# Two convolution taps placed later, a copy placed before an update, and two PSUM homes exchanged in the KDA stage

## What is computed

```
q = l2norm(silu(conv4(x @ Wq)));  k = l2norm(silu(conv4(x @ Wk)));  v = silu(conv4(x @ Wv))
g = -exp(A_log) * log1p(exp(clip(x @ Wfa @ Wfb + dt_bias, -20, 20)));  beta = sigmoid(x @ Wb)
for each token i and head:                      # 16 heads of 128
    state = state * exp(g_i)
    state = state + (beta_i * k_i) (v_i - k_i . state)
    o_i   = q_i . state
out = rmsnorm(o) * norm_w * sigmoid(x @ Wga @ Wgb) @ Wo
```

## Time and profile before

| | us |
|---|---|
| median of 3 runs | 7070.68 (7065.52 to 7080.7) |
| the profiled execution | 7072.26 |
| its span | 7070.4 |
| loop over 32 KDA blocks, 2534 to 5158 us in the span | 2624 |
| PE busy in the span | 5833.4 (83%) |
| DVE, ACT, POOL busy | 3136.2, 2846.3, 2260.3 |
| granted clock of PE, mean of the span; of the loop | 0.885; 0.92 |

### The profile page before, as it was taken

How to read it: one execution, slowest core, us unless ns; L and a number is a source line. 1 busy time by engine, 2 the same in 40 slices (tenths; PEclk the granted TensorE clock), 3 DMA queues, 4 the chain that set the end, 5 groups by cost and what they waited for, 6 DMA issues and landing times. The chain is left out here.

```text
span 7070.4 us, 126135 instructions
## 1 busy us (share of the span) xinstructions
PE 5833.4 (83%) x52984; PEld 3848.7 (54%) x52984; DVE 3136.2 (44%) x4540; ACT 2846.3 (40%) x5154; POOL 2260.3 (32%) x1583
## 2 busy tenths in 40 slices
PE   6877789754899678888888888888889997888999
PEld 5666566543566345555555555555544445665444
DVE  5545333323332255555555555655532115664211
ACT  2322334333343354554454455454531115664111
POOL 4444000001000046555566655656522220001222
PEclk8988788877778789999999999999989998889999
DMA  0000000000000000000000000000021110002111
GB/s 26 3 3 31 0 0 0 14 0 29 0 0 0 9 20 15 15 15 22 15 15 15 15 15 15 22 15 15 15 82 42 42 40 1 0 0 78 42 41 46
DMA packets 60570, 136.55 MB, mean 19 GB/s; under 512 B 11638, under 2 KB 24054, under 8 KB 58842
## 3 DMA queue, kind: packets, MB, share of 16 engines
q1 hardware_dynamic: 60122, 129.79, 5.5%
HBM read 127.26 MB, written 2.50 MB: 18 GB/s over the span
## 5 line engine op out<-in xcount | busy, mean ns | idle before, releaser
L569 PE MATMUL ps<-moe_xn_all,moe_w 128*128 128x512 f32 x1792 | 810.3, 595 | 0.0
L1688 POOL TENSOR_TENSOR kda_g<-kda_g,kda_f 128x512 f32<-128x512 f32 x225 | 422.7, 1879 | 500.6 <-DVE kda_rows L1680 493.9
L569 PEld LDWEIGHTS ps<-moe_xn_all,moe_w 128*128 128x128 f32 x1792 | 341.2, 191 | 423.9 <-issue 423.3
L682 DVE TENSOR_TENSOR moe_h<-moe_silu,ps 128x512 f32<-128x512 f32 x224 | 154.1, 688 | 935.8 <-ACT moe_silu L624 928.8
L1511 DVE SCALAR_TENSOR_TENSOR kda_cv<-kda_pre,kda_w_front,kda_cv 128x1024 f32<-128x1024 f32 x297 | 545.2, 1836 | 3.6
L1399 PE MATMUL ps<-kda_xn_all,kda_w_front 128*128 128x512 f32 x808 | 428.1, 679 | 128.3 <-ACT kda_cv L1438 103.5
L624 ACT ACTIVATE moe_silu<-ps 128x512 f32<-128x512 f32 x224 | 133.7, 597 | 986.4 <-PE ps L569 986.4
L525 POOL TENSOR_TENSOR moe_h<-moe_h,moe_cb 128x512 f32<-128x512 f32 x176 | 233.5, 1327 | 696.6 <-DVE moe_h L682 696.6
L579 PE MATMUL ps<-moe_h,moe_w 128*128 128x512 f32 x896 | 420.4, 592 | 0.0
L1680 POOL TENSOR_TENSOR kda_rows<-kda_q,kda_f 128x512 f32<-128x512 f32 x225 | 322.3, 1433 | 199.8 <-remote 174.0
L1399 PEld LDWEIGHTS ps<-kda_xn_all,kda_w_front 128*128 128x128 f32 x808 | 167.6, 219 | 321.6 <-issue 176.8
(11 more groups left out here) (506 smaller groups left out, 12804.3 us busy)
## 6 DMA issues: line engine op xcount, KB each, us to landing
kda_col<-kda_beta SPq DMA_DIRECT2D x34, 512.0 KB, 4.3
moe_w<-in_Mw SPq DMA_DIRECT2D x6, 2816.0 KB, 20.1
moe_cb<-kda_beta SPq DMA_DIRECT2D x64, 256.0 KB, 3.2
kda_w_front<-in_Kw SPq DMA_DIRECT2D x34, 455.0 KB, 4.9
moe_cb<-kda_beta SPq DMA_DIRECT2D x32, 224.0 KB, 2.9
kda_w_out<-in_Kw SPq DMA_DIRECT2D x32, 192.5 KB, 4.9
moe_cb<-kda_beta SPq DMA_DIRECT2D x32, 192.0 KB, 2.8
moe_cb<-kda_beta SPq DMA_DIRECT2D x32, 160.0 KB, 2.7
```

The lines of the kernel that those rows point to most:

```text
L569: last = nc.tensor.matmul(ps_gu[u % 2][r], w13[:, k, i, r], n.xn[:, k, cols(c)], start=k == 0, stop=k == KD - 1)
L1688: step(nc.gpsimd.tensor_tensor(halves(decay_g[:], h, 0), halves(decay_g[:], h, 0), second_total, ALU.mult))
```

## The change

On DVE, the three taps of q stood together ahead of everything else in the block. Now one stays there, one stands behind the write of `t[:, :, 1]`, and one behind `a_rows(2)`; the clip moves behind the write of `t[:, :, 0]`. At level 3, the copy `tail.inner(1)` stands ahead of `update(3)`, and the tap `f.tap(2, 1)` behind it.

On PE, the second projection of `ahead` writes banks 0 and 1 in place of 6 and 7 and waits for `n.aq_in_sb >= 2` (ACT has read the last scores from these banks) in place of `m.head_read >= 2`. The second output projection writes banks 6 and 7 in place of 0 and 1 and waits for `m.head_read >= 2`. ACT and DVE read from the new places. The number of instructions is the same on every engine.

```diff
-        OUT = (TAIL, SCORES)
+        HEAD, OUT = (FRONT, SCORES), (TAIL, FRONT)
@@ head_pe @@
             def project(i):
                 if i == 0:
                     pe.wait_ge(m.w_front_in, 16)
-                else:
-                    pe.wait_ge(m.head_read, 2)
-                project_pe(w, quad, i, m.head_ready)
+                project_pe(w, quad, i, HEAD[i], m.head_ready)
@@ chain_pe @@
             last.then_inc(n.bg_ready, 1)
+            pe.wait_ge(n.aq_in_sb, 2)
             ahead.project(1)
             pe.wait_ge(n.ylog, 1)
             tail.out(0)
-            pe.wait_ge(n.aq_in_sb, 2)
+            pe.wait_ge(m.head_read, 2)
             tail.out(1)
@@ chain_dve @@
             a_rows(1)
-            for j in range(CONV - 1):
-                f.tap(0, j)
+            f.tap(0, 0)
             dve.wait_ge(n.diag_ready, 1)
...
             nc.vector.tensor_tensor(t[:, :, 1], lt[:, 0], ident, ALU.add).then_inc(n.t_ready, 1)
-            f.clip()
+            f.tap(0, 1)
             dve.wait_ge(n.x_ready, 1)
             nc.vector.tensor_tensor(t[:, :, 0], ps_x, ident, ALU.add).then_inc(n.t_ready, 2)
+            f.clip()
             tail.inner(0)
             masks(1)
             a_rows(2)
+            f.tap(0, 2)
             f.tap(1, 0)
...
             f.tap(2, 0)
+            tail.inner(1)
+            update(3)
             f.tap(2, 1)
-            update(3)
-            tail.inner(1)
             f.tap(2, 2)
```

More of the change, by code:

```diff
@@ L1388, in project, with project_pe @@
                     pe.wait_ge(m.w_front_in, 16)
-                else:
-                    pe.wait_ge(m.head_read, 2)
-                project_pe(w, quad, i, m.head_ready)
+                project_pe(w, quad, i, HEAD[i], m.head_ready)
             return Calls(project=project)
-        def project_pe(w, quad, i, done):
+        def project_pe(w, quad, i, bank, done):
             for hf in range(2):
@@ L1398, in project_pe @@
                     at = K_QKV + (i * KD + k) * P
-                    last = nc.tensor.matmul(psum(g, FRONT + hf, BANK), w[:, at:at + P],
+                    last = nc.tensor.matmul(psum(g, bank + hf, BANK), w[:, at:at + P],
                                             xn_all[:, k, bass.ds(quad * QUAD + hf * BANK, BANK)], start=k == 0,
@@ L1410, in project @@
                 pe.wait_ge(m.dec_in_sb, 1)
-                project_pe(w, quad, 2, m.proj_ready)
+                project_pe(w, quad, 2, FRONT, m.proj_ready)
             def values():
@@ L1434, in front_pe, with project_act @@
             return Calls(decay=decay, project=project, squares=squares, values=values)
-        def project_act(i, w, done):
-            nc.scalar.activation(pre[i % 2][:, :, CONV - 1:], two(FRONT), ACT.Copy).then_inc(done, 1)
-            nc.scalar.activation(cv[i % 2][:], two(FRONT), ACT.Identity,
+        def project_act(i, w, bank, done):
+            nc.scalar.activation(pre[i % 2][:, :, CONV - 1:], two(bank), ACT.Copy).then_inc(done, 1)
+            nc.scalar.activation(cv[i % 2][:], two(bank), ACT.Identity,
                                  scale=w_vec(w, K_CONV + i * CONV + CONV - 1)).then_inc(done, 1)
@@ L1444, in project @@
                 act.wait_ge(m.head_ready, i + 1)
-                project_act(i, w, m.head_read)
+                project_act(i, w, HEAD[i], m.head_read)
             return Calls(project=project)
@@ L1453, in project @@
                 act.wait_ge(m.silu_ready, 1)
-                project_act(2, w, m.proj_read)
+                project_act(2, w, FRONT, m.proj_read)
             def decay():
```

## The result

| | before | after |
|---|---|---|
| median in us, 4 runs each | 7068.1 (7061.63 to 7080.7) | 6865.37 (6865.04 to 6876.2) |
| the profiled execution, its span | 7072.26, 7070.4 | 6865.6, 6863.6 |
| loop over 32 blocks | 2619.69 | 2424.26 |
| granted clock of PE: span; loop | 0.885; 0.92 | 0.892; 0.94 |

A forecast was written before the change was run, and what follows sets the result against it. No engine is full; a block is a chain of hand-overs closed by a barrier. 25 normal blocks at 7.7 us, 7 after a jump at 3.6, and 4 us ahead of the loop give 222 off 7072: 6850, range 6785 to 6950.

The forecast's parts named there:

- The end: End of all 32 blocks: second projection follows the transposes, POOL is last, barrier opens 3.7 us earlier (3.0 to 4.3).
- The third rival: Block end: the wait before `out(1)` becomes the old 3.03 us, end gives about 1.4, total 6924; chance 0.04.
- The start of a normal block: Start of 25 of 32 blocks: mask and state product come earlier, 3.4 us gained (1.5 to 5).
- The milestone: Sign at level 0: PE's L1761 starts without waiting for the mask, 5.9 us after block start instead of 9.9.
- the 0.2 of the sum: Block start: loss from PE starting at the low clock after idling across the barrier, 0.2 us (0 to 1.5).
- A block after a jump: Start of 7 of 32 blocks: moved tap and clip delay the copy to `d`, 0.9 us lost (0 to 2.3).
- Level 3: Level 3, all 32 blocks: copy ahead of update brings level 4's mask earlier, 0.8 us gained (-0.2 to 2.0).
- I take off half of 1.6: Level 3: half of the mask's 1.6 us gain deducted because the lower clock may hit level 4's products and transposes.
- The first: Whole loop: the clock holds, normal blocks give 9.4 us and those after a jump 4.4, total 6802; chance 0.25.
- The second: Whole block: only the end counts, POOL's port turns and the clock eat the rest, total 6950; chance 0.15.
- The slower one: Whole loop: PE's idle pieces keep the clock down, near 0.82 or below, 1.7 us a block lost, 7126; chance 0.04.

The follow-up runs named there:

- the two idle matmuls: Changed kernel plus two 128x512 matmuls with unread results on PE behind the scores of level 4: 6819.69 us.
- the banks alone: Kernel before with only the exchanged PSUM banks and PE waits, DVE's order as before: 6900.97 us against 7066.37.
- level 3 alone: Kernel before with only the level-3 copy ahead of the update and the tap behind it: 7096.14 us, ratio 1.0036.
- the first experiment: Kernel before with only the exchanged PSUM banks and PE waits: 6900.97 us, ratio 0.977.
- the best version: Changed kernel plus two unread matmuls at level 3 and two at the block's end, with one tap of q and one of k later: 6769.23 us.
- the taps alone: Kernel before with only the two moved taps of q and the clip, banks and level 3 as before: 7021.39 us, ratio 0.9934.
- the filling at the end: Changed kernel plus two unread 128x512 matmuls on PE behind a block's last output projection: 6862.74 us.

## Why the prediction was right, and where not

**The end, forecast 3.7 us:** 3.72, as worked out: no gap, the 3.60 of an output projection, POOL last, the barrier no slower. The third rival (the wait before `out(1)` is felt) didn't come: L1612 follows L1397 with no gap.

**The start of a normal block, forecast 3.4 less 0.2 for a cold start:** 3.14. That the size was right is luck: two errors cancel. I let POOL block one DVE instruction or a little more, and took 0.7 off for a clock that falls while PE waits for the copy. In fact the moved tap was blocked in all 32 blocks, and PE's new wait (1.0 to 1.6 us, the low end of my 1 to 3) lowered the clock in none of them: L1582 took 1.16 us and L1759 of level 1 1.15. By "SBUF — State Buffer" of the Trainium skill, section Who interferes with whom, the shared ports go to DVE or to POOL for a whole instruction, and the other waits until it is over. The trace agrees: a tap of 1.26 us took 2.29 here beside POOL. The prediction gave 3.2 for the start if that happened each time, before any cost of a lower or cold clock; the blocks least delayed by their cold start gave 15.60 - 12.08 = 3.5. The milestone was wrong: L1759 of level 0 starts 7.4 to 8.5 us into a block, not 5.9, since L1380 and L1792 ahead of it run cold after the barrier (2.4 to 3.75 us and 1.98). DVE felt it too, for its diagonal waits for L1792 (1.32 us idle in the block above). With a warm start L1759 came at 5.8. So a cold start costs PE 1.5 to 2.6 us, but most of it lies beside DVE. The 15 blocks whose product starts at 7.4 have the state product at 12.08, no later than with a warm start (12.09); the nine at 8.2 or later have it at 13.12. So the 0.2 of the sum was 0.4.

**A block after a jump, forecast -0.9 at its start:** -1.2. It shortened by 2.96 us where 3.6 were forecast, and by 4.0 less than the others, as said.

**Level 3, forecast 0.8:** 0.12 by the sections, and 4 us of 32 blocks, 0.13, by the run without it. This is the step that failed: "I take off half of 1.6". The working had it all (the mask at 1.6 us sooner, PE waiting there for "2 us or so" in place of the copy, the lower clock on three groups of the path) and then only half its price. The gap was 2.53 us, the clock fell behind it in 31 of the 32 blocks, and the price was 1.5 (from the two idle matmuls), as large as the gain. In all 32 blocks (0.80 - 0.16) x 32 = 20 us of the 23 by which the loop's forecast of 218 was too high; the starts of normal blocks and of those after a jump are 1.5 and 2.2, and the end gives 1.5 back.

The median missed the forecast by 15 us; without the 5.5 that fell ahead of KDA it would be 21.

**The rivals.** The first, a clock that holds (6802), was wrong for the changed kernel, but its 1.6 us for level 3 is what the two idle matmuls gave (0.41 + 1.15 = 1.56, the sections to update 3 and to update 4 against before; 6819.69 in all). The second, only the end (6950), was wrong; the banks alone, though, are worth 165 us and not 122. The slower one needed a clock of 0.82 in the loop, and it rose to 0.94. But its mechanism is real: level 3 alone came out slower by it, at 0.90.

What stays open: which gaps the clock answers. The same wait for the mask, 2.53 us, gave 1.97 us for the next group in some blocks and 1.69 in others, and in one block after a jump 1.15, with update 4 only 9.75 us behind update 3. The wait of 1.6 us for the transposes of v had both outcomes as well. The cold and the warm start of the first experiment are two blocks of the same order. The runs show what each arrangement does, and I can't say beforehand which it will be.

## What to carry to other kernels

When an instruction is moved ahead to end a wait, ask where the engine stops next: a gap that only moves one group further is worth nothing, and where the clock falls behind it, less than nothing. A gap of PE that can't be closed can be filled with matmuls that nobody reads, if they end before the awaited data is there: two paid 46 us, four nothing. Measure such edits together as well as alone, since the place where the clock is low depends on the whole loop.

## What the runs showed of the hardware

- A matmul of 128x512 in fp32 stands as two rows of the trace and takes 0.92 us at the full clock (four of them, x8, took 3.70), so four did not fit a gap of 2.53 us and two did.
- Making PE busier made the program faster: in the best version PE is busy for 38 us more than in the changed kernel, and the loop is 86 us shorter.
- The length of a gap alone did not decide the clock. At the start of a block a wait of 2.9 us was followed by a cold group in all 10 warm-started blocks of the taps alone and all 16 of the filling at the end, and one of 1.0 to 1.6 us in none of the changed kernel's 32. But behind a wait of 1.6 us ahead of the transposes of v, with the tap of v moved, these ran cold in 19 blocks and warm in 13.
- A barrier with 4 us of idle PE didn't always mean a cold start: behind the same 3.91 us L1380 took 1.96 in one block and 3.75 in the next.
